# One stage of a four-layer gated transformer kernel rebuilt: part of it moved into the stage before, its two halves run one behind the other

## What is computed

```python
# layer 1, cross attention (latent): its tail stands ahead of the changed stage
x = x + tanh(g_xattn[1]) * latent_attention(layernorm(x), ctx)
# layer 1, feed forward: base product plus a gated low rank product
logits = sigmoid(xf @ router_W.T)                 # 32 gates, each used twice, plus biases
top_v, top_i = top_k(logits, 8)
gating = sparse / sum(sparse) * 8
mid = xf @ A.T                                    # 64 wide
x = x + tanh(g_ffn[1]) * (xf @ base_W.T + 2 * (mid * gating) @ B.T)
# layer 2, score attention: queries and keys come from ctx, not from x
scores = (qp @ kp.T) / 8 * qc_score               # qc_score = layernorm(x)
x = x + tanh(g_xattn[2]) * softmax(where(mask, -inf, scores))
# layer 2, feed forward: router first
probs = softmax(layernorm(x) @ router_w.T)        # 8 experts, 2 chosen, 64 places each
```

## Time and profile before

| | us |
|---|---|
| median of 3 runs | 1165.95 |
| the profiled execution | 1167.08 |
| its span, first to last instruction | 1165.3 |
| TensorE busy | 1018.5 (87%) |
| VectorE busy | 711.2 (61%) |
| ScalarE busy | 479.0 (41%) |
| GpSimd busy | 194.3 (17%) |
| `mid`, first instruction to the last one | 748.9 to 825.8 |

### The profile page before, as it was taken

One profiled execution on the slowest core, in us unless ns is written; L12 is line 12 of the kernel. 1 busy time (PEld: TensorE's weight loads), 2 busy tenths in 40 slices (PEclk: granted clock), 3 DMA queues, 4 the chain that ended last, 5 costly groups with the idle time before them and its releaser, 6 DMA issues. The chain is left out here.

```text
span 1165.3 us, 23228 instructions
## 1 busy us (share of the span) xinstructions
PE 1018.5 (87%) x9280; PEld 834.9 (72%) x9280; DVE 711.2 (61%) x1747; ACT 479.0 (41%) x853; POOL 194.3 (17%) x163
## 2 busy tenths in 40 slices
PE   8979989679998899999699999674696999989997
PEld 4747777567776687878577877564595777678886
DVE  0667778767776565554566666465635577754544
ACT  1447777513334344443143333233341343434443
POOL 4100000010001233343320000041101000123342
PEclk8999999979999899999899999875797899888999
DMA  8600000000001122332000000100100000122232
GB/s 289 223 2 3 3 1 3 1 1 2 3 18 34 54 89 80 111 93 66 8 2 2 2 2 2 37 1 0 37 1 1 2 3 18 33 84 90 81 110 68
DMA packets 17707, 48.29 MB, mean 41 GB/s; under 512 B 3072, under 2 KB 5248, under 8 KB 17472
## 3 DMA queue, kind: packets, MB, share of 16 engines
q1 hardware_dynamic: 17600, 46.80, 12.5%
HBM read 45.61 MB, written 1.05 MB: 40 GB/s over the span
## 5 line engine op out<-in xcount | busy, mean ns | idle before, releaser
L1566 POOL TENSOR_TENSOR p_WML<-p_raw,p_WMH 128x768 fp32r<-128x768 f32 x56 | 103.6, 1850 | 174.1 <-ACT p_WMH L1651 168.6
L1682 ACT ACTIVATE p_AHI<-p_A 128x512 fp32r<-128x512 f32 x62 | 39.2, 632 | 169.0 <-DVE p_A L1764 169.0
L1764 DVE TENSOR_TENSOR p_A<-p_A,PS 128x512 f32<-128x512 f32 x62 | 42.7, 688 | 85.4 <-PE PS L1614 84.7
L1287 ACT ACTIVATE p_E<-PS 128x768 f32<-128x768 f32 x64 | 51.7, 807 | 87.8 <-PE PS L1138 87.8
L1392 DVE TENSOR_REDUCE p_mx<-PS 128x2 f32<-128x512 f32 x64 | 44.1, 689 | 60.1 <-PE PS L1102 60.0
L736 PE MATMUL PS<-p_FT,p_PTS 128*128 128x128 f32 x512 | 64.0, 278 | 16.1 <-DVE XNS L888 14.8
L736 PEld LDWEIGHTS PS<-p_FT,p_PTS 128*128 128x128 f32 x512 | 59.9, 192 | 22.0 <-DVE p_PTS L924 20.6
L1768 DVE TENSOR_TENSOR p_ALO<-p_A,p_AHI 128x512 fp32r<-128x512 f32 x62 | 44.8, 723 | 43.3 <-ACT p_AHI L1682 43.3
L82 PE MATMUL PS<-p_WMH,p_AHI 128*128 128x256 f32 x224 | 63.1, 282 | 3.5 <-DVE p_ALO L1768 3.3
L84 PE MATMUL PS<-p_WMH,p_ALO 128*128 128x256 f32 x224 | 62.6, 279 | 0.0
L83 PE MATMUL PS<-p_WML,p_AHI 128*128 128x256 f32 x224 | 62.5, 279 | 0.0
(11 more groups left out here) (498 smaller groups left out, 3297.2 us busy)
## 6 DMA issues: line engine op xcount, KB each, us to landing
p_raw<-in_moe SPq DMA_DIRECT2D x56, 448.0 KB, 3.3
p_fr<-in_fold SPq DMA_DIRECT2D x16, 480.0 KB, 4.4
p_raw<-in_wpack SPq DMA_DIRECT2D x8, 416.0 KB, 5.5
p_early_raw<-in_moe SPq DMA_DIRECT2D x6, 448.0 KB, 3.2
CP<-in_consts SPq DMA_DIRECT2D x1, 1725.0 KB, 9.5
XS<-in_x SPq DMA_DIRECT2D x1, 1024.0 KB, 14.4
W2R<-in_ffn SPq DMA_DIRECT2D x4, 256.0 KB, 3.4
p_W3R<-in_ffn SPq DMA_DIRECT2D x4, 256.0 KB, 3.3
```

The lines of the kernel that those rows point to most:

```text
L1287: act.activation(E[:, n % 4], PS[:, ST:ST + 2, 0:384], ACT.Exp, scale=scale).then_inc(s["ex"], 1)
L1566: g.tensor_tensor(WML[:, n % RING, :], raw[:, i % RAW, 0:SEL], WMH[:, n % RING, 0:SEL].bitcast(F32), ALU.subtract).then_inc(s["w_lo"], 1)
L1764: v.tensor_tensor(A[:, b, :], A[:, b, :], PS[:, GS_BANK, :], ALU.mult).then_inc(s["ag"], 1)
```

## The change

In the latent stage, ScalarE now makes half 0's layer norm of the next stage between its last exponentials (new tile use of `HN`), TensorE turns it between `output(14)` and `output(15)`, both engines split it, and TensorE makes half 0's router product (96 columns) as the last thing in the stage, into PSUM bank 2. `mid` starts with half 0's gates ready to be computed and reads bank 2.

In `mid` half 0 goes ahead: `query_keys(0)`, `base(0)`, then half 1's transposes, `lora_turned(0)`, half 1's router product, `lora(0)`, `query_keys(1)`, `base(1)`. ScalarE makes all the layer norms of the score step (VectorE made those of half 0 before), and for the last layer norm ScalarE makes half 0 and two tiles of half 1, VectorE two tiles. Sixteen matmuls whose results nobody reads (`warm`, 512 columns, bf16) stand on TensorE ahead of the last transposes; they wait for the second exponential of half 1. VectorE ranks half 0 before it looks at half 1's logits. GpSimd makes `nbias` for both halves.

```diff
+                        pe.wait_ge(s["mxd"], NP)
+                        for t in range(TT):
+                            pe.wait_ge(s["nx"], t + 1)
+                            for k in range(KC):
+                                m = pe.transpose(PS[:, SC + k, t * P:(t + 1) * P], HN[:, t, k * P:(k + 1) * P], ident)
+                        m.then_inc(s["nx_t"], 1)
                         output(NQ - 1)
+                        pe.wait_ge(s["nx_lo"], KC)
+                        ... # mm3 with 96 columns, 8 times, into PS[:, ST, ...]
# ScalarE, latent stage
+                            if 26 <= n < 26 + TT:
+                                if n == 26:
+                                    act.wait_ge(s["ln_nb"], 2)
+                                    act.wait_ge(s["mk"], NT)
+                                t = n - 26
+                                act.activation(HN[:, t, :], XS[:, t, :], ACT.Identity, ...).then_inc(s["nx"], 1)
# mid, banks and TensorE
-                QP, TR, BASE, MR, MT, SC = (((7, 3), (0, 1)), (0, 4), (4, 0), (6, 2), (7, 3), (6, 2))
+                QP, TR, BASE, MR, MT, SC = (((7, 3), (0, 1)), (0, 0), (4, 0), (2, 6), (7, 3), (6, 2))
+                        query_keys(0)
+                        base(0)
                         transposes(1, s[1]["n1"], s[1]["t1_done"], TR[1])
+                        lora_turned(0)
                         pe.wait_ge(s[1]["t1_lo"], KC)
                         mid_router(1)
+                        lora(0)
+                        query_keys(1)
                         pe.wait_ge(s[1]["q_raw"], 2)
                         base(1)
+                        lora_turned(1)
+                        scores(0)
                         lora(1)
                         scores(1)
+                        pe.wait_ge(s[0]["res"], TT)
+                        pe.wait_ge(s[1]["es"], 2)
+                        warm(pe, WARM["mid"], bank=BASE[0])
+                        transposes(0, s[0]["n3"], s[0]["t3_done"], BASE[0])
+                        transposes(1, s[1]["n3"], s[1]["t3_done"], BASE[1], s[1]["n3d"])
# mid, VectorE
+                        gating(0)
+                        split_lo(1, s[1]["t1_hi"], s[1]["t1_lo"], TR[1])
+                        low_rank_lo(0)
+                        gating(1)
+                        low_rank_out(0)
+                        low_rank_lo(1)
+                        stats(0, 0)
+                        low_rank_out(1)
+                        stats(1, 0)
...
+                        split_lo(0, s[0]["t3_hi"], s[0]["t3_lo"], BASE[0])
+                        v.wait_ge(s[1]["ln_rstd"], 2)
+                        norm(1, s[1]["n3d"], 2)
+                        split_lo(1, s[1]["t3_hi"], s[1]["t3_lo"], BASE[1])
                         for h in range(HALVES):
                             route_first(h)
-                        for h in range(HALVES):
                             route(h)
```

More of the change, by code:

```diff
@@ L1980, in _ @@
                         output(NQ - 2)
-                        output(NQ - 1)
+                        pe.wait_ge(s["mxd"], NP)
[4 more added lines that the diff above has]
+                        m.then_inc(s["nx_t"], 1)
+                        output(NQ - 1)
+                        pe.wait_ge(s["nx_lo"], KC)
+                        for t in range(TT):
+                            for k in range(KC):
+                                m = mm3(pe, PS[:, ST, t * 96:t * 96 + 96], pair(HH, HL, slice(None), k, slice(t * P, t * P + P)),
+                                        weight("l1f", KC, k, 256, 352), t == 0 and k == 0, k == KC - 1, skip=True)
+                        m.then_inc(s["nx_mr"], 1)
                     @block.scalar
@@ L2126, in _ @@
                         context_lo(NQ - 1)
+                        for k in range(KC):
+                            v.wait_ge(s["nx_hi"], k + 1)
+                            v.tensor_tensor(HL[:, k, :], PS[:, SC + k, :], HH[:, k, :].bitcast(F32), ALU.subtract).then_inc(s["nx_lo"], 1)
                         residual(B - 1)
@@ L2133, in mid @@
             with Phase() as ph:
[L2134 removed]
+                s = [ph.halves("n1 n2 n3 n3d ln_nb ln_stats ln_aggr ln_eps ln_rstd t1_done t1_hi t1_lo t3_done t3_hi t3_lo "
                                "qp q_raw q_hi q_lo mr base ex la lr lb top rep ne sp su rs ga mt m_hi m_lo lora res "
@@ L2183, in _, with transposes @@
                                 stats_gpsimd(g, s[h], h, i)
-                                if h:
-                                    bias_gpsimd(g, s[h], h, i)
+                                bias_gpsimd(g, s[h], h, i)
                     @block.tensor
                     def _(pe):
-                        def transposes(h, ready, done, bank):
+                        def transposes(h, ready, done, bank, other=None):
                             for t in range(TT):
-                                pe.wait_ge(ready, t + 1)
+                                if other is None:
+                                    pe.wait_ge(ready, t + 1)
+                                elif t < 2:
+                                    pe.wait_ge(other, t + 1)
+                                else:
+                                    pe.wait_ge(ready, t - 1)
                                 for k in range(KC):
@@ L2210, in base, with lora_turned @@
                                         t % 2 == 0 and k == 0, False, skip=True)
-                        def lora(h):
+                        def lora_turned(h):
                             for t in range(TT):
@@ L2217, in lora @@
                             m.then_inc(s[h]["mt"], 1)
-                            if h:
-                                scores(0)
+                        def lora(h):
                             wh, wl = weight("l1b")
@@ L2293, in _, with query_keys_hi @@
                                 act.activation(QR[h][:, r, :], PS[:, QP[h][r], :], ACT.Identity, bias=const("qkb2")[:, r:r + 1]).then_inc(s[h]["q_raw"], 1)
-                        for h in range(HALVES):
+                        def query_keys_hi(h):
                             for r in range(2):
@@ L2320, in _, with norm @@
                     def _(v):
-                        def norm(h, done):
-                            for t in range(TT):
+                        def norm(h, done, tiles):
+                            for t in range(tiles):
                                 g = TT * h + t
```

81 lines of the change are left out of this document (37 added, 44 removed).

## The result

The changed kernel took 1154.93 us (median of 4 runs, 1154.36 to 1156.42), against 1166.58 for the kernel before (4 runs, 1165.56 to 1167.45). The ratio is 0.9881, its 95% interval 0.9858 to 0.9904: faster by 1.2%, clear of the noise. The profiled execution took 1155.46 us against 1167.08. The forecast was 1154.7, with 1150.0 to 1160.5 as its range.

A forecast was written before the change was run, and what follows sets the result against it. No one engine bounds the stage: TensorE, then VectorE, then a relay of serial pieces. -6.3 (tail and P within), -1.6 and -3.35 make -11.2, so 1155.9 from the profiled 1167.08, forecast 1154.7 as median; range 1150.0 to 1160.5.

The forecast's parts named there:

- Tail: End of the latent stage: half 0's added transposes, split and router product go into idle gaps; -0.5 us, bounds -0.6 and +1.3.
- P: Start of VectorE's low part of half 1's low-rank input, 777.01 before; forecast at 771.7, -5.3 us, tail's -0.5 included.
- P to the end of VectorE's dense stretch: VectorE's dense stretch ends at 792.8 instead of 799.07 despite a new wait behind GpSimd; -6.3 us with P included.
- To the logits: From the end of VectorE's dense stretch to TensorE's logits: 4.55 us instead of 6.18; -1.6 us.
- Ranks: End of the stage: half 0's ranking runs under half 1's logits, with a wait for ScalarE's exponential in return; -3.35 us.
- Nothing behind: Behind the barrier nothing changes: the next stage starts on a slow TensorE before and after.
- rival 1: TensorE's high clock holds through half or all of the logits; 2.4 to 4.9 us less, about 1151; chance 0.13.
- rival 2: GpSimd and VectorE lock each other: six GpSimd instructions each hold VectorE up by 0.6; 3.8 later, 1158.5 us; chance 0.10.
- rival 3: TensorE stays at the low clock ahead of P: P at 779.4, about 1165 us or a loss; chance 0.08.
- rival 4: The halves don't come apart: all of P slides with a late `gating(1)`, only Ranks and Tail stay; 1161 us; chance 0.04.

The follow-up runs named there:

- side by side: Changed kernel with its latent tail and end kept, but the two halves run side by side through the middle as in the kernel before; 1157.81 us.
- weights first, norm on VectorE: Changed kernel with GpSimd subtracting the four weight tiles before half 1's queries and keys, and half 0's second norm back on VectorE; 1158.06 us.
- tail back: Changed kernel with half 0's norm, transposes, split and router product moved back from the latent tail to the start of `mid`; 1166.62 us.

## Why the prediction was right

- **Tail, -0.5.** Against the last matmuls ahead of the edit (L1930 at 736.34 before, L1931 at 738.54 after, so 2.20 to take off), the residual starts 0.38 earlier. The reason was right too: with the gap empty again, the clock falls in `output(15)` and VectorE's wait is 2.19 once more.
- **P, -5.3.** P less 2.20 is 771.57, forecast 771.7; the measure from the latent start says -5.68. The course there was a little different: the low clock took the last third of half 1's router product, all of `lora(0)` and queries and keys, and `base(1)` ran at the high clock, as assumed. The prediction put the gain down to the two edits without asking what either is worth alone; the runs say that the stagger alone would have been a loss.
- **P to the end of VectorE's dense stretch, together -6.3.** The last aggregate ends 794.46 + 0.36 - 2.20 = 792.62 (forecast 792.8, before 799.15). The late statistics at GpSimd, written down as a new wait before the run, are there: they start at 775.53 (forecast 775.7), and the norms at 777.51 (777.7). VectorE's wait was 1.25, not 0.8, because it came 0.5 earlier: it didn't wait for `lora(1)`. What the prediction missed is that this wait cancelled the ScalarE norm's gain wholly. It booked 1.34 for the norm and 1.4 for wait and slower products as separate entries, which is right in the sum and hides that the edit is worth nothing as built (19.45, and 19.17 with it undone).
- **To the logits, -1.6.** Measured -1.67; the extra matmuls are 0.84 of it, or 0.92 against the other runs' 5.94. That the number came out is luck: two errors cancel. First, the prediction had half 1's transposes at the low clock, 2.0 us. The extra matmuls brought the clock up, and from the first of these transposes to the logits it took 1.02. Second, the prediction let the transposes start behind the first norm, some 2.6 us behind the last aggregate. They started 3.40 behind it (798.22 less 794.82), because VectorE makes its two norms (from 797.76 on) only behind the low part of half 0. With the clock low, as the prediction assumed it, the piece is 6.86 and the term -0.83.
- **Ranks, -3.35.** Measured -3.31, and -3.32 by the run that undid it.
- **Nothing behind.** The piece to the next stage was 0.23 shorter; the rest of the program 0.4 slower. The term is not quite nothing: `capacity_experts` itself took 0.39 more from its first matmul to that of the stage behind it (52.88 before, 53.27 after). The low clock lasted 3.6 us into it before and 4.9 now, and over the runs its length goes with this: 52.52 with 2.9 (side by side), 53.65 with 5.7 (weights first, norm on VectorE).

The rivals. The clock did not hold in the changed kernel (rival 1): it was up over both halves' last transposes and fell 0.12 us ahead of the logits. In other versions it held for up to 15 of the 48 matmuls, worth 1.4 us. The lock between GpSimd and VectorE (rival 2) showed in one small instruction: L2405 took 0.47 us instead of 0.17 beside GpSimd's first subtractions, and the low part at 773.77 took 0.68 beside its weight tiles as before. TensorE at the low clock (rival 3) did not come, but the run with the tail back shows half of it: 3.5 us of P's lateness. The halves came apart (rival 4). Three of the rivals' numbers don't follow from their own terms: six times 0.6 is 3.6 and not 3.8 (rival 2), P at 779.4 is 7.7 later where the bound says 7 (rival 3), and the route and tail terms alone give 1162.1 and not 1161 (rival 4).

## What to carry to other kernels

Cut the path into pieces that add up, between instructions that exist in every version: here each untouched piece but the logits repeated within 0.2 us, while medians of the kernel moved by 3. When work moves off the busiest engine, ask first whether that engine waits at this point for something else; if it does, both must be mended or neither pays (norm and queue order: 0.28 lost and 0.05 gained alone, 1.15 gained together). A reordering may be worth having only behind another edit: undo each alone before calling it a gain.

## What the runs showed that I had not expected

- The stagger alone makes P 4.74 us later, with the tail it makes it 2.62 earlier.
- The granted clock falls after 0 to 15 of the logits' 48 narrow matmuls, by how early they begin in a high stretch of 6.83 us that came at the same place in every version with tail, stagger and extra matmuls (225.4 to 225.8 us behind the start of S). Neither a filled gap nor wide matmuls among them made it longer.
- Unchanged stages vary between executions by more than most edits are worth: one took 156.6 to 162.7 us, another 142.2 to 145.1.
